# A transformer block on one core: where the last batch's output projections, the left-over parts of the attention outputs and the rounding of a weight matrix stand in the order

## The reference, cut to what matters

```
x = x + attention(layernorm(x))      # 16 heads of 16, softmax over 512 keys
x = x + ffn(layernorm(x))            # silu(x W1) * (x W3), Hadamard transform, W2
x = x + memory(layernorm(x))         # gated exponential smear along the sequence
x = x + ffn(layernorm(x))
# attention: out = softmax(Q K^T / 4) V;  return out @ Wo.T + bo
```

## Time and profile before

| what | us |
|---|---|
| median of 3 runs | 563.42 (562.08 to 564.31) |
| the profiled execution's own time | 561.39 |
| its span, first to last instruction | 559.6 |
| PE busy, of the span | 547.4 (98%) |
| DVE, ACT, POOL busy | 385.8, 311.7, 192.6 |

### The profile page before, as it was taken

How to read it: one execution, slowest core, us unless ns; L and a number is a source line. 1 busy time by engine, 2 the same in 40 slices (tenths; PEclk the granted TensorE clock), 3 DMA queues, 4 the chain that set the end, 5 groups by cost and what they waited for, 6 DMA issues and landing times.

```text
span 559.6 us, 8472 instructions
## 1 busy us (share of the span) xinstructions
PE 547.4 (98%) x2932; PEld 368.2 (66%) x2932; DVE 385.8 (69%) x727; ACT 311.7 (56%) x581; POOL 192.6 (34%) x221
## 2 busy tenths in 40 slices
PE   8999999999999998999999999999999999999997
PEld 5553343344435433468888888888888888888887
DVE  6898988898898899836475555756886437364433
ACT  3668889876987787753333233366775323323231
POOL 4795367562546252520122012422332012102120
PEclk9999999999999999999999999999999999999999
DMA  7465440230023030021122221210000202223121
GB/s 218 109 197 168 141 134 3 72 127 32 3 97 132 2 152 4 2 75 21 19 43 33 34 42 18 43 18 1 0 2 0 34 12 43 64 39 76 25 52 39
DMA packets 74554, 32.54 MB, mean 58 GB/s; under 512 B 59608, under 2 KB 67800, under 8 KB 74128
## 3 DMA queue, kind: packets, MB, share of 16 engines
q1 hardware_dynamic: 73292, 30.93, 20.6%
q10 hardware_dynamic: 1220, 1.07, 0.6%
HBM read 10.89 MB, written 5.24 MB: 29 GB/s over the span
## 4 chain that ended last, share of the span: by engine, by line
PE 87%; DVE 5%; ACT 3%; issue 2%; SPq 2%; DMA 1%; ACTq 0%; POOL 0%; DVEq 0%
PE PS L426 85%; DVE mxr L1141 2%; SPq L384 2%; PE PS L437 1%; ACT PR L966 1%; DMA xf<-PR 1%; PE PS L624 1%; DMA ring<-mT 1%; ACT AOh L838 0%; DVE PR L1280 0%; DVE OT L1206 0%; ACT PR L1034 0%; ACT XNs L1028 0%; ACTq L928 0%; DVE X L1315 0%
## 5 line engine op out<-in xcount | busy, mean ns | idle before, releaser
L426 PE MATMUL PS<-xTh,ring 128*128 128x512 f32 x608 | 187.5, 391 | 0.0
L1141 DVE TENSOR_REDUCE mxr<-PS 128x1 f32<-128x512 f32 x256 | 162.9, 681 | 24.0 <-PE PS L426 23.1
L966 ACT ACTIVATE PR<-PS 128x512 f32<-128x512 f32 x256 | 138.0, 602 | 29.8 <-PE PS L426 29.3
L426 PEld LDWEIGHTS PS<-xTh,ring 128*128 128x128 f32 x608 | 113.4, 188 | 24.5 <-issue 1.7
L426 PE MATMUL PS<-xTl,ring 128*128 128x512 f32 x304 | 109.8, 390 | 0.0
L838 ACT ACTIVATE AOh<-PR 128x512 fp32r<-128x512 f32 x72 | 45.5, 632 | 112.0 <-DVE PR L1280 106.5
L426 PE MATMUL PS<-ring 48*128 48x512 f32 (+1 forms) x512 | 99.4, 451 | 4.5 <-DVE mxr L1141 2.8
L1280 DVE TENSOR_TENSOR PR<-PR,PS 128x512 f32<-128x512 f32 x64 | 43.5, 679 | 66.2 <-PE PS L426 45.5
L426 PEld LDWEIGHTS PS<-ring 50*128 50x128 f32 (+1 forms) x512 | 41.4, 185 | 71.0 <-ACT PR L966 43.5
L1402 POOL TENSOR_TENSOR xTl<-xf,xTh 128x512 fp32r<-128x512 f32 x30 | 41.9, 1410 | 134.1 <-ACT xTh L838 134.1
L1133 DVE TENSOR_TENSOR AOl<-PR,AOh 128x512 fp32r<-128x512 f32 x72 | 55.2, 767 | 45.5 <-ACT AOh L838 45.4
(11 more groups left out here) (142 smaller groups left out, 728.8 us busy)
## 6 DMA issues: line engine op xcount, KB each, us to landing
ring<-qh SPq DMA_DIRECT2D x48, 128.0 KB, 2.8
xf<-PR SPq DMA_DIRECT2D x112, 32.0 KB, 1.9
ring<-ql SPq DMA_DIRECT2D x24, 128.0 KB, 2.8
ring<-weight_scratch SPq DMA_DIRECT2D x3, 1024.0 KB, 4.8
Vp<-qf SPq DMA_DIRECT2D x96, 32.0 KB, 1.9
weight_scratch<-in_w SPq DMA_DIRECT2D x2, 1024.0 KB, 6.7
X<-in_x SPq DMA_DIRECT2D x3, 512.0 KB, 4.8
out<-X SPq DMA_DIRECT2D x6, 256.0 KB, 2.4
```

The source lines that it names most:

```text
L426: return nc.tensor.matmul(dst, lhsT, rhs, start=start, stop=stop, skip_group_check=True)
L966: nc.scalar.activation(PR[:, j % 8, :], PS[:, kq_bank(j), :], ACT.Exp, scale=HD ** -0.5)\
L1141: nc.vector.tensor_reduce(mxr[:, S % 2, blk, TT * p + t:TT * p + t + 1], PS[:, QK0 + i % 3, :], AX.X, ALU.max, negate=True).then_inc(max_d ...
```

## The change

The order is set by tables of step numbers, and they are edited:

```diff
-OUT_AT = ((20,), (24, 26))
-V_AT = ((22,), (28, 30))
-MAX_AT = 3
+OUT_AT = ((20,), (28, 30))
+V_AT = ((22,), (24, 26))
+LAST_OUT_AT = ((12, 14), (16, 18))
+MAX_AT, LAST_MAX_AT = 3, 20
+AO_AT, LAST_AO_AT = STEPS - 1, 21
...
+        def out_at(b):
+            return LAST_OUT_AT if b == BATCH - 1 else OUT_AT
+        def turned_at(K):
+            S = (K + LEAD) // 8 - 1
+            if S == LAST_GROUP - 1:
+                return S if K % STEPS == LAST_MAX_AT else None
+            return S if K % 8 == MAX_AT and S < LAST_GROUP else None
...
                 if s // 8 == 0:
                     pe.wait_ge(x_f, 2 * (b + 1))
-                elif s // 8 < 3 and b < BATCH - 1:
+                elif b == BATCH - 1:
+                    pe.wait_ge(x_done, 2 * b - 2 + 2 * (s == LAST_MAX_AT))
+                elif s // 8 < 3:
                     pe.wait_ge(qk_f, 4 * b + 2 * (s // 8))
-                elif s // 8 == 3:
-                    pe.wait_ge(*((x_done, 2 * b) if b else (w2h_done, 3)))
+                else:
+                    pe.wait_ge(*((v_copied, 2 * b + 4) if b else (w2h_done, 3)))
...
-                    pe.wait_ge(*((v_copied, 2 * b + 2) if b > 1 else (w2h_done, 4)))
+                    pe.wait_ge(*((x_done, 2 * b - 2) if b > 1 else (w2h_done, 4)))
                     ln_transpose(0, MB)
...
-                if s == OUT_AT[0][0] and b:
-                    pe.wait_ge(aol_done, 2 * b)
-                    pe.wait_ge(mt_ready, turned)
-                    for part in range(2):
-                        out_projection(0, part)
-                if s in OUT_AT[1] and b:
-                    if s == OUT_AT[1][0]:
-                        pe.wait_ge(*((v_copied, 2 * b + 3) if more else (x_done, 2 * b - 1)))
-                    out_projection(1, OUT_AT[1].index(s))
+                for half in range(2):
+                    at = out_at(b)[half]
+                    if b and s in at:
+                        if s == at[0]:
+                            pe.wait_ge(aol_done, 2 * b)
+                            pe.wait_ge(mt_ready, turned)
+                            if half and not more:
+                                pe.wait_ge(x_done, 2 * b - 1)
+                        for part in range(2) if len(at) == 1 else (at.index(s),):
+                            out_projection(half, part)
...
                     if s == V_AT[1][0]:
-                        pe.wait_ge(mt_ready, turned)
+                        pe.wait_ge(v_copied, 2 * b + 3)
...
-                if s == OUT_AT[1][-1] + 2:
+                if s == (LAST_AO_AT if b == BATCH - 1 else AO_AT):
                     act.wait_ge(aof_ready, 2 * b + 1)
...
-                            if s == OUT_AT[half][-1] + 1:
+                            if s == out_at(b)[half][-1] + 1:
                                 add_attention(b - 1, half)
...
-                if b == BATCH - 1 and SPLIT_AT <= s < SPLIT_AT + 8:
-                    w_split_hi((s - SPLIT_AT) // 4, (s - SPLIT_AT) % 4)
+                if b == BATCH - 1:
+                    for w, at in ((W_UP, SPLIT_AT), (W_LIN, 26)):
+                        if at <= s < at + 4:
+                            w_split_hi(w, s - at)
...
                 if s == 6 and b:
+                    output_lo(2 * b - 1)
+                if s == 7 and b:
                     output_lo(2 * b)
-                if s == OUT_AT[1][-1] + 3:
+                if s == LAST_AO_AT + 1 and b == BATCH - 1:
                     output_lo(2 * b + 1)
```

More of the change, by code:

```diff
@@ L365, in _ @@
                         weights_in(W_LIN)
[L366 to L369, removed]
+                    S = turned_at(STEPS * b + s)
+                    if S is not None:
+                        max_rows(S)
                     if b == 0 and s == 24:
@@ L693, in _ @@
                     weigh_values((K - 3) // 2)
-                S = (K + LEAD) // 8 - 1
-                if s % 8 == MAX_AT and S < LAST_GROUP:
+                S = turned_at(K)
+                if S is not None:
                     turn_maxima(S, b, s)
@@ L1007, in _ @@
                             qk_split(b + 1, n)
-                if s % 8 == MAX_AT and (K + LEAD) // 8 - 1 < LAST_GROUP:
-                    max_evacuate((K + LEAD) // 8 - 1)
+                S = turned_at(K)
+                if S is not None:
+                    max_evacuate(S)
             act.wait_ge(aof_ready, 2 * BATCH)
```

## The result

| | before | after |
|---|---|---|
| median | 562.75 us (4 runs) | 574.42 us (4 runs) |
| profiled execution | 561.39 us | 574.89 us |
| its span | 559.6 us | 573.1 us |
| its mean granted clock of PE | 1.000 | 0.982 |

The ratio is 1.0195, with a 95% interval of 1.0153 to 1.0237; ratios leave out disturbed executions, here one of 581.4 us, without which the median after is 574.0. The forecast was 569.0 us, with a range that ended at 572.5. So the change made the kernel slower, as forecast, but by some 11 us (11.7 between the medians of the table) instead of 5.6, and the time lies above the range.

The account below looks back on a forecast made before the run. PE bounds batches 1 and 2, DVE in a loop with PE batch 3's steps 4 to 19, ACT the tail. 6.55 + 1.35 - 2.1 + 0.2 - 0.5 + 0.4 = +5.9, taken as 563.42 + 5.6 = 569.0 us; range 562.5 to 572.5.

Parts of the forecast that it names:

- The place and the chain: Step 4, batches 1 to 3: DVE waits 2.7 us for POOL's left-over, then PE about 2 us in step 6.
- (a): Rival: the stall at step 4 is absorbed, the sum is -0.65 to 0, 563 us; chance 0.13.
- (b): Rival: stall absorbed, and batch 3's projections fit into PE's waits of 0.44 us, 560.5 us; chance 0.07.
- (c): Rival: ACT's rounding at step 5 is held too, PE waits again in following periods, +10, 573 us; chance 0.12.
- (d): Rival: PE's clock falls to 1.2 GHz after each 2.1 us stall, 9.7 us more for three, 579 us; chance 0.03.
- The stall's term: Late left-over at step 4: 2.1 us lost in batches 1 and 2 each, 2.35 in batch 3, sum +6.55 us.
- Projections and tail: Batch 3: output projections in steps 12 to 19 cost +1.35 us; ACT's tail from step 20 saves 2.1.
- the transfer of the maxima: Tail of batch 3: step 24's scores may wait for it; up to 0.5 us could come back, 0.2 taken.
- Turn at step 27, against step 31: Step 27's turn no longer waits for an addition, -0.5 us; addition and ACT's rounding fall into step 31, +0.4.
- has cover: Tail: W3's rounding, some 4.2 us of DVE, starts three steps later at no cost, since DVE idles 5.22 us.
- Everything but the left-over: The whole change without the stall at step 4: worth -0.65 us.

Follow-up runs that it names:

- e4: The changed kernel with POOL's left-over of the half before at step 4, ahead of both placements, instead of step 6: 568.25 us, ratio 1.0135.
- e3: The changed kernel with ten unread matmuls on PE in step 6 of batches 1 to 3, ahead of the late wait: 568.67 us, ratio 1.0107.
- e8: e1 with W3's rounding back at steps 23 to 26, as in the kernel before: 565.2 us, ratio 1.0056.
- e1: The changed kernel with POOL's left-over of the half before moved back to step 1, ahead of the placements: 559.45 us, ratio 0.9946.
- e2: The kernel before with only the left-overs of batches 1 to 3 moved as in the change; projections and W3 stay: 577.26 us, ratio 1.0255.
- e5: The changed kernel with POOL's left-over of the half before at step 5, between the two placements: 571.48 us, ratio 1.0184.

## Why the prediction missed, point by point

- **The place and the chain: right.** DVE's turn into `AOf` at step 4 waits for POOL's left-over, 2.95, 2.60 and 2.58 us against 2.70; PE waits for the maxima behind it, 2.37, 2.19 and 2.54 against 2.1, 2.1 and 2.35. Rivals (a) and (b), the stall absorbed, are out: PE waits, and e4's batches 1 and 2 lose more than their waits at full clock. So is (c) as the reason, though its 573 us came nearest to the measured time: there PE would have waited again for ACT, and e3, with the same late rounding, loses 8.2 us where (c) had 2.7 and 1 for each stall, 11.1. In the kernel after, ACT and DVE are busy little more than half of the long stretch behind the stall while PE leaves no gap.
- **The failing step: PE's clock, which the sum put at nothing, and which stood only in rival (d), given 0.03.** It fell behind all three stalls. The argument set against it was that the clock was 1.00 in stretches whose longest waits were 0.44 us; that says nothing of waits of 2 us. The text itself says that the trace speaks neither for nor against, and the chance of 0.03 has no other ground. It priced it at +9.7 us (a period at half speed costs its 3.23 us once more, three times); measured are 8.4 us in the profiled execution. That the two are close is in part luck: they are made up of one long stretch and two short ones, and not of a period each. The Trainium skill's rule ("TensorE: Matmul & The Clock Gate", section "Part 1: The HAM clock gate"), that the clock is halved for an idle engine and given back after sustained work, was cited and then outvoted. The trace agrees with its direction, a fall behind idle time. With (d) in the sum, for waits of this length, the forecast would have been 579; the measured 574.4 lies between that and 569.0.
- **The stall's term, mis-sized a little.** 6.55 us forecast, 7.7 to 8.2 measured by e3, inside its bounds of 4.5 and 8.1 but for the last tenth. PE did wait a little more than worked out, and batch 3 gave nothing back: its loss is 2.69 in e3, DVE's full wait.
- **Projections and tail: more gain.** Scores of step 20 against step 11 in batch 3 came 1.13 us later (forecast 1.35), with periods of 3.24 in steps 12 to 17 (230.06 to 233.29, 236.54 and 239.78), as the prediction had them. In the tail ACT took 12.39 us (243.30 to 255.69) against 15.22 before, a gain of 2.83 where 2.1 less 0.2 was forecast: it worked without a gap from its first pair on, and at 0.49 us an exponential (9.79 for 20), where the prediction had counted 0.515. The timeline of ACT in the tail of the kernel after (compare):

```profile
243.30 1.09 ACT L983 ACTIVATE PR<-PS 128x512 f32<-128x512 f32 x2 [0.33 <-PE PS L439]
...
245.38 0.61 ACT L855 ACTIVATE AOh<-AOf 128x512 fp32r<-128x512 f32 x1
245.90 9.79 ACT L983 ACTIVATE PR<-PS 128x512 f32<-128x512 f32 x20
```

The timeline of PE in the kernel after, the scores of step 24 (compare):

```profile
247.12 0.74 PE L439 MATMUL PS<-ring 50*128 50x512 f32 x4 [0.52 <-DMA ring<-mT]
```

20 exponentials stand in one unbroken row. PE's scores of step 24 do wait 0.52 us for the transfer of the maxima, as feared, but ACT has work queued and never notices: that term is 0, not 0.2.
- **Turn at step 27, against step 31.** -0.5 + 0.4 forecast; -0.56 measured between the stalls. So step 31 costs nothing that shows, and the +0.4 was not there.
- **W3: the step "has cover" was wrong in its reason.** The prediction read DVE's 5.22 us of idle time before the last turn and said that starting W3 three steps later costs nothing, which held: 2.27 us of idle time are left before that turn (257.04). What it missed is that the later start is needed: W3 at its old steps costs some 6 us (e8). The kernel before had W3 there without a wait of PE. Timelines of before, DVE's turn of the group's output, then PE's weighed values that need it:

```profile
233.76 0.72 DVE L1206 STREAM_TRANSPOSE OT<-PS 128x512 f32<-128x512 f32 x1
...
235.38 1.07 PE L426 MATMUL PS<-PR,Vp 128*32 128x512 f32 x8
```

Counted from the turn of maxima at step 11 (213.89 before, 214.91 in e8), PE is ready for these values 1.65 us sooner in e8 (234.75 against 235.38), and DVE makes its turn 2.07 us later (236.85 against 233.76). PE follows the turn's start after 0.86 us in e8 and came 1.62 us behind it before, so the slack was 0.76 us. 1.65 + 2.07 - 0.76 is 2.96, the wait in e8's row. The projections in the tail had been the cover, but they are only half of it: DVE's own work on W1 and W3 also runs later.
- **Everything but the left-over.** e1 at full clock lies 2.6 us under the kernel before in the median (558.5 to 558.9 against 560.5 to 561.7), where the prediction had -0.65.

**The sum as measured**, on the profiled executions: stall 8.2, clock 8.4, between the stalls -0.6, from step 11 of batch 3 to the loop's end -1.7, before batch 1's stall -0.1: +14.2 at the loop's end, +13.5 at the end of the execution. The 0.7 between these two I have not traced. The medians differ by less, 11.7: the profiled execution of before lies 1.4 us under its median, at full clock where about half of the later executions of that kernel had less, and that of the kernel after 0.5 over its own.

**What stays open.** Why the half clock lasted some 14 us behind one stall and 3.4 behind another. It is not the batch and not the length of the wait: the long stretch stands behind batch 1's stall in the kernel after, behind those of batches 2 and 3 in e2, and waits of 2.22 and 2.24 us in e2 had 3.4 and 14 us. PE's work is of the same kinds behind all of them, and the records leave hardly a gap in the long stretches. No run here tells them apart. What exactly lets the clock fall after a wait as short as 1.18 us in one place, and not after 1.02 and 0.82 in two others, is open too. That the clock is the cause of the 8.4 us is shown (e3); when it falls, and for how long, is not.

## What to carry to other kernels

When an operation is moved, ask not what waits it has, but who waits for it: a buffer with one copy turns a late reader on one engine into a wait on another engine's queue, and everything behind that wait pays. Price a new stall of TensorE of a microsecond or more twice, once at its length and once for the clock that may fall behind it; products that nobody reads can keep the clock up where the stall can't be avoided (e3: 8.4 us less behind the same three stalls, and medians 5 to 6 us apart). And when an edit has cover, check whether another part of the same change is that cover.

## What the runs showed of the hardware

- The granted clock fell to 1.2 GHz behind waits of PE of 2.2 to 2.5 us, of 1.5 to 1.9 us (e5), and once of 1.18 us where one of 0.44 us stood before it (e4). It also fell in the prologue of e1's profiled execution (mean 0.996), while five others of e1 had 0.999 or 1.000.
- Stretches at half clock lasted 3.4, about 10 (batch 3 of e5), about 14 and about 17 us (e4). In the 14 us of the kernel after PE's records stand back to back. Waits of 2.22 and 2.24 us in one execution (e2) were followed by 3.4 and by 14 us.
- Three DVE waits of 2.7 us cost 8.2 us with PE kept at work (e3) and 16.6 us without (the kernel after, profiled execution).
- A cast of 128x512 on DVE went from 0.41 us (the kernel after) to between 1.07 and 1.48 us (e8), and a subtraction from 0.69 to 1.66, beside POOL's two-input operations, which themselves went from 1.28 up to 1.71 us.
